# Attention scores and values of 16 groups: the next group's load cut into 14 issues spread over the step

## What is computed

```
scores = einsum('bqhd,bkhd->bhqk', Q, K) / sqrt(16)      # Q, K, V: (2, 2048, 16, 16)
scores = where(causal, scores, -inf)
attn   = softmax(scores, axis=-1)
out    = einsum('bhqk,bkhd->bqhd', attn, V)
x_out  = x + attention_1(norm(x)) + layer(norm(x))        # the layer holds attention_2 and the experts
```

## Time and profile before

| | us |
|---|---|
| median of 3 runs | 2648.76 (2633.55 to 2656.8) |
| profiled execution, its own time | 2634.57 |
| its span | 2632.8 |
| stage B, first to last score matmul | 273.2 to 1939.6 |
| engines busy over the span | PE 86%, DVE 71%, ACT 57%, POOL 22% |

### The profile page before, as it was taken

How to read it: one execution, slowest core, us unless ns; L and a number is a source line. 1 busy time by engine, 2 the same in 40 slices (tenths; PEclk the granted TensorE clock), 3 DMA queues, 4 the chain that set the end, 5 groups by cost and what they waited for, 6 DMA issues and landing times. The chain is left out here.

```text
span 2632.8 us, 45311 instructions
## 1 busy us (share of the span) xinstructions
PE 2277.3 (86%) x15785; PEld 1263.7 (48%) x15785; DVE 1866.1 (71%) x5760; ACT 1507.5 (57%) x3172; POOL 576.3 (22%) x490
## 2 busy tenths in 40 slices
PE   5986899999999999999999999999948512999994
PEld 3553344444444434444444444444426502899994
DVE  3536787978878889889888789797605642666662
ACT  2541576767767777777677677676840101445551
POOL 0001101010110110110100000100003265677775
PEclk9995798988989889989889899898978755999997
DMA  5994805415244154253252441541124403566663
GB/s 174 290 244 149 189 6 70 51 26 67 34 50 58 18 68 53 30 67 47 38 67 29 56 58 26 67 53 24 19 63 146 128 27 123 127 141 142 128 130 86
DMA packets 153968, 221.68 MB, mean 84 GB/s; under 512 B 57204, under 2 KB 116158, under 8 KB 145328
## 3 DMA queue, kind: packets, MB, share of 16 engines
q1 hardware_dynamic: 137136, 199.99, 38.3%
q0 software_dynamic: 16640, 19.25, 5.1%
HBM read 139.22 MB, written 89.39 MB: 87 GB/s over the span
## 5 line engine op out<-in xcount | busy, mean ns | idle before, releaser
L659 ACT ACTIVATE probs<-s_banks 128x512 f32<-128x512 f32 (+3 forms) x2560 | 1185.3, 538 | 442.8 <-PE s_banks L610 284.4
L696 DVE TENSOR_REDUCE rowmax<-m_banks 128x1 f32<-128x512 f32 x1536 | 967.0, 683 | 100.5 <-PE m_banks L621 93.4
L610 PE MATMUL s_banks<-qs,ks 50*128 50x512 f32 (+3 forms) x2560 | 872.5, 443 | 69.1 <-DMA qs<-mrows 53.3
L621 PE MATMUL m_banks<-ks,qs 48*128 48x512 f32 (+3 forms) x2560 | 839.6, 451 | 26.1 <-PEq L86 20.4
L639 PE MATMUL v_bank<-probs,vs 128*32 128x512 f32 (+3 forms) x5120 | 650.8, 583 | 1.1 <-ACT probs L659 0.4
L610 PEld LDWEIGHTS s_banks<-qs,ks 50*128 50x128 f32 x2560 | 422.7, 196 | 460.7 <-ACT probs L659 373.2
L693 DVE CUSTOM_DVE_ANT_0 unused<-m_banks,c_maskq 128x128 bf16<-128x128 f32 (+3 forms) x1024 | 465.9, 486 | 151.1 <-issue 147.8
L621 PEld LDWEIGHTS m_banks<-ks,qs 48*128 48x128 f32 x2560 | 417.8, 200 | 305.5 <-DVE rowmax L696 143.9
L552 POOL CAST nparts<-negmax 128x16 fp32r<-128x16 f32 x64 | 12.7, 198 | 1328.0 <-DVE negmax L702 1328.0
L1327 PE MATMUL e_banks<-w_parts,hid_parts 128*128 128x256 f32 x1536 | 188.8, 284 | 1.3 <-DVE hid_parts L1246 0.7
L1327 PEld LDWEIGHTS e_banks<-w_parts,hid_parts 128*128 128x128 f32 x1536 | 185.5, 192 | 2.0 <-DVE hid_parts L1246 1.1
(11 more groups left out here) (172 smaller groups left out, 1712.2 us busy)
## 6 DMA issues: line engine op xcount, KB each, us to landing
w<-in_L_ffn_fc_w SPq DMA_DIRECT2D x32, 1024.0 KB
qs<-q_scratch SPq DMA_DIRECT2D x96, 256.0 KB, 14.5
ks<-k_scratch SPq DMA_DIRECT2D x96, 256.0 KB, 16.2
q_scratch<-parts SPq DMA_DIRECT2D x64, 256.0 KB, 4.6
k_scratch<-parts SPq DMA_DIRECT2D x64, 256.0 KB, 4.5
xin_scratch<-rden POOLq DMA_DIRECT2D x16, 528.0 KB, 26.8
xin<-xin_scratch SPq DMA_DIRECT2D x16, 528.0 KB
v_scratch<-vt SPq DMA_DIRECT2D x16, 512.0 KB, 7.7
```

The lines of the kernel that those rows point to most:

```text
L610: ins = pe.matmul(bank, ks[rows, slot, h // 2, k * P:(k + 1) * P], qs[rows, slot, h // 2, q * CH + first:(q + 1) * CH], start=True, stop=n ...
L621: pe.matmul(room(("M", NM * group + n))[:, 0:width], qs[rows, slot, h // 2, t * P:(t + 1) * P], ks[rows, slot, h // 2, c * CH:c * CH + wid ...
L659: act.activation(probs[:, n % PR, 0:width], s_banks[:, (NS * group + n) % SRING, 0:width], ACT.Exp, scale=SCALE).then_inc(p_ready, 1)
L696: dve.tensor_reduce(out, scores, AX.X, ALU.max).then_inc(m_used, 1)
```

## The change

The load's one entry in the order becomes 14, at key tiles 1 to 14, each of which issues one of the same 14 DMAs, in the same order and through the same queue. The wait for `p_used` stays ahead of the first. Stage A's load of group 0 issues its 14 pieces in one go, as before.

```diff
+PIECES = 14
+
+def load_piece(queue, g, n, drams, keep):
     q_dram, k_dram, v_dram = drams
     qs, ks, v_in, loaded = keep
-    slot = g % SLOTS
-    for half in range(2):
-        for n in range(3):
-            at = slice(half * HALF + n * HD, half * HALF + (n + 1) * HD)
...
-            sp.dma_start(qs[at, slot].bitcast(F32), q_rows).then_inc(loaded[slot], 16)
-            sp.dma_start(ks[at, slot].bitcast(F32), k_rows).then_inc(loaded[slot], 16)
...
+    slot, half, place = g % SLOTS, n // 6, n // 2 % 3
+    if n < 12:
+        dram, rows, part = ((q_dram, qs, (0, 0, 1)), (k_dram, ks, (0, 1, 0)))[n % 2]
+        at = half * HALF + place * HD
+        queue.dma_start(rows[at:at + HD, slot].bitcast(F32),
+                        dram[part[place], g].rearrange("(a b) r t -> b r a t", b=2)[half]).then_inc(loaded[slot], 16)
+    else:
+        values = v_dram[g // (B * HG), g // HG % B, :, :, g % HG * (GH * HD):(g % HG + 1) * (GH * HD)]
+        tiles = slice((n - 12) * (S // P // 2), (n - 11) * (S // P // 2))
+        queue.dma_start(v_in[:, slot, tiles], values[:, tiles]).then_inc(loaded[slot], 16)
...
-                    load_group(sp, 0, (q_dram, k_dram, v_dram), keep)
+                    for n in range(PIECES):
+                        load_piece(sp, 0, n, (q_dram, k_dram, v_dram), keep)
...
-        if n == LOAD_AT and g + 1 < G:
-            order.append(("L", g + 1, 0))
+        if LOAD_AT <= n < LOAD_AT + PIECES and g + 1 < G:
+            order.append(("L", g + 1, n - LOAD_AT))
...
-            def load(g):
-                if g >= SLOTS:
+            def load(g, n):
+                if n == 0 and g >= SLOTS:
                     sp.wait_ge(p_used, AHEAD + NT * (g - SLOTS + 1))
-                load_group(sp, g, (q_dram, k_dram, v_dram), keep)
+                load_piece(sp, g, n, (q_dram, k_dram, v_dram), keep)
...
-                        load(group)
+                        load(group, n)
```

More of the change, by code:

```diff
@@ L55 @@
 SLOTS = 2
-def load_group(sp, g, drams, keep):
+PIECES = 14
+def load_piece(queue, g, n, drams, keep):
     q_dram, k_dram, v_dram = drams
     qs, ks, v_in, loaded = keep
-    slot = g % SLOTS
-    for half in range(2):
-        for n in range(3):
-            at = slice(half * HALF + n * HD, half * HALF + (n + 1) * HD)
-            q_rows = q_dram[(0, 0, 1)[n], g].rearrange("(a b) r t -> b r a t", b=2)[half]
-            k_rows = k_dram[(0, 1, 0)[n], g].rearrange("(a b) r t -> b r a t", b=2)[half]
-            sp.dma_start(qs[at, slot].bitcast(F32), q_rows).then_inc(loaded[slot], 16)
-            sp.dma_start(ks[at, slot].bitcast(F32), k_rows).then_inc(loaded[slot], 16)
-    tiles = v_dram[g // (B * HG), g // HG % B, :, :, g % HG * (GH * HD):(g % HG + 1) * (GH * HD)]
-    for n in range(0, S // P, S // P // 2):
-        sp.dma_start(v_in[:, slot, n:n + S // P // 2], tiles[:, n:n + S // P // 2]).then_inc(loaded[slot], 16)
+    slot, half, place = g % SLOTS, n // 6, n // 2 % 3
[8 more added lines that the diff above has]
+        queue.dma_start(v_in[:, slot, tiles], values[:, tiles]).then_inc(loaded[slot], 16)
 def stage_a(nc, x, scratch, const, keep):
```

## The result

The changed kernel takes 2554.3 us (median of 4, 2536.9 to 2557.5) against 2641.2 us (2629.7 to 2656.8): a ratio of 0.9672, interval 0.9628 to 0.9716, or 87 us less. The forecast was 2530, the range 2490 to 2605.

A forecast was written before the change was run, and what follows sets the result against it. Bound: late rows of maxima, held behind the load in SP's queue, making PE wait at tile 16 and costing clock. Steps 1 to 14 save 106.7 us, step 0 saves 2: 2634.6 - 108.7 = 2525.9, stated as 2530, range 2490 to 2605.

The forecast's parts named there:

- Rows of tile 16: Steps 1 to 14: rows of maxima issued at +20.8 in 4.90 us, so the 42 us of waits at tile 16 go.
- The load's landing: Next group's load complete at +39, ahead of its first M matmul at +41.7 in tile 17; slack 2.7 us.
- A step at full clock: Steps 1 to 14 without the wait: 37.9 + 56.4 = 94.3 us, taken as 94.5.
- The clock in steps 1 to 14: Clock falls in half of the steps, some 11 us low, 0.4 us lost per us: 2.2 us a step.
- Step 0: Beside POOL's fill, 11.3 us of waiting become 9 at the next group's first M: a gain of 2 us.
- Step 15, the term put at nothing: Last step, which loads nothing: its time was to stay as profiled, adding no gain or loss.
- Rival N: Steps 1 to 14: the gap alone caused the clock's fall, so none remains; 94.5 us a step, 2495 us; chance 0.17.
- The row of step 8: Evidence cited for Rival N: in step 8 the first low-clock window lies inside the wait at tile 16.
- B: Narrow tiles 13 to 15 bring the clock down every step, some 15 us: 100.5 us a step, about 2580; chance 0.20.
- C: Load lands some us late, so the wait moves to the next group's first M: about 2635 or 2594 us; chance 0.07.
- D: Values' pieces still need 25 us to land, first M waits 12 us each step: slower, 2788 us; chance 0.04.

The follow-up runs named there:

- second experiment: Changed kernel with all 12 pieces of queries and keys at tile 1 and only the two values' pieces behind the rows, at tile 9: 2559.3 us, ratio 0.9723.
- first experiment: Changed kernel with eight pieces issued together at key tile 1 and six at tile 9, nothing spread: 2543.5 us, ratio 0.9666.
- third experiment: Changed kernel with all 14 pieces of the load issued behind the rows, at tile 9: 2814.6 us (one run).
- fourth experiment: The changed kernel unaltered, run again for another profile: 2543.8 us, ratio 0.9633.

## Why the prediction was right, and where it was off

*Rows of tile 16, right, by a row misread in part.* Issued at +20.8 in 5.0 us, 42 us of waits gone. The prediction compared the row of 16 issues in the earlier trace rows (21.86 us) with 8 in 4.90. But the 16 are the rows of two chunks, the second eight wait until +37 for their own copy, and in step 15, where nothing holds them, they take 21.34 us as well. What shows that SP was held is the first issue alone, in the kernel before (step 2, then step 3):

```profile
515.04 12.58 SPq L480 DMA_DIRECT2D qs<-mrows  x1
...
609.67 1.05 SPq L72 DMA_DIRECT2D v_in<-v_scratch  x2
618.60 14.59 SPq L480 DMA_DIRECT2D qs<-mrows  x1
```

Both issues end at +35.4, just behind the landing of the eleventh piece (+34.8 in step 2), and the other seven follow, so that the last row goes out at +39.8. In step 3 the values' pieces go out in 1 us and the rows bear all of the hold. That it takes the values' pieces was inferred; the second experiment shows it, and the first that no spreading is needed.

*The load's landing, right.* +39.5 for my +39, the first M at +41.5 for my +41.7. The load was in time in every step, but not always with 2 us to spare: in step 3 it landed at +41.6 (issue at 610.2 and 12.9 us, start 581.5), too late by 0.1 us for a first M at +41.5; no wait came of it because the low clock had put that M off to +43.1. In the first experiment's step 3 it was +41.3 against a first M at +41.5. The third experiment shows the price beyond.

*A step at full clock, right.* 94.2 us; the sum gave 94.3 and I took 94.5.

*The clock in steps 1 to 14, too small.* In the first profile the low time is 99 us, 7.1 a step, for my 5.5 (half of the steps by 11 us). At 41 us lost over 14 x 94.2, 0.42 for each us, the rate was right. Ten of 14 steps had a fall, not seven, since there is a second place, behind tile 19 at +49, that no step of the kernel before had shown. So 97.1 us a step for my 96.7: 6 us. In the second profile (the fourth experiment) 12 of 14 steps had a fall, with 143 us of low time, 10.2 a step: 98.3 us a step, 22 us over the sum. The term was mis-sized, by little in one execution and by a factor of nearly two in the other.

*Step 0.* The wait became 8.1 us for my 9; the gain was 0.5 us for my 2, and 5 in the second profile.

*Step 15, the term put at nothing.* "Step 15 and the other stages stay" took one profiled execution for the rule. I had read its 3.4 us fall and used it for the others, but did not ask what a longer one would cost there. In four of the twelve profiles of kernels other than the one of before, its clock was low for 50 us or more (one of them had step 15 itself altered), in two of the kernel before for 3.4 us each; what decides this stays open. In the first profile this made 23.2 of the 31.7 us by which the execution fell short of my sum (108.7 against 77.0); 6 came from the clock, 1.5 from step 0 and 1.0 from the other stages. In the second, 20 us above my sum, step 15 had no part: the clock of steps 1 to 14 made 22, the other stages 1, and step 0 gave back 3. Both executions lost to the clock most of what the sum lacked, the first in step 15, the second in steps 1 to 14.

*The rivals.* Rival N (no falls once the gap is gone: 2495) is what the advice of the Trainium skill ("TensorE: Matmul & The Clock Gate", section "Why this matters for your kernels") gave. The measurements differ: in the fourth experiment every step from 3 to 15 fell with no gap ahead of it. The kernel before had shown it too. In step 1 the wait is from 424.9 to 427.5, and all of it is at the low clock, behind a window at 1.00 and with PE busy throughout:

```profile
421.40:424.80 3.40, 3.40 (x40) 2.71 (x40) 3.10 (x30) 2.63 (x11) 0.42 (x2) 1.00 0.99 140
424.90:427.50 2.60, 0.00 (x0) 0.00 (x0) 1.22 (x8) 0.13 (x1) 0.00 (x0) 0.50 0.01 3
```

So the wait cannot have brought the clock down there. In nine of the 14 steps it fell at +38.1 to +38.6, within 0.4 us of the wait's beginning at +38.2. The row of step 8 that the prediction held for N is one of them. With tiles 14, 15 and 19 filled, the time is 2493.6; that this is N's figure is chance, as it holds 10 us or more from POOL's fill and 12 matmuls a step that N did not have. B had the right place, the tiles ahead of tile 16; it said every step, some 15 us and 100.5 us a step, and the second profile came near it with 12 steps of 14, 12 us each and 98.3. C and D did not come.

## What to carry to other kernels

Look in the timeline of the issuing engine for issues that take 10 us where others take half a us: the queue is closed, and small urgent transfers should be issued ahead of the piece that closes it. A merged row of many issues does not show this; narrow the window to the first of them. When a short PE wait goes, count the low-clock time behind it too, and then look at what stands just ahead of each fall: here 12 superfluous matmuls a step, at under 0.1 us each, removed them. Where runs of one kernel spread by 20 us, a term "stays as it is" from a single profile is not safe.

## What was not expected of the hardware

The clock fell in stretches where the PE row shows no idle time over 0.3 us, at two fixed places: behind tiles 14 and 15, and behind tile 19. (That row counts a matmul as busy from start to modelled end; how full the array is does not show in it.) Putting 8 matmuls of 512 columns at the first place lengthened a step by 0.6 us and saved about 30 us in all; 4 more at the second, with POOL's fill moved, left steps 1 to 14 without a fall. Once low, the clock came back after 3.4 to 27 us in most steps, but in step 15 it stayed down for 54.6 us, and in the run with added matmuls through all of the 91.3 us that were left of the step, with the PE row busy throughout. A load of 12 pieces of 32 rows of 8 KB did not hold up SP for long (0.42 us an issue at the median, 1.5 at most in the second experiment); with two pieces of 256 KB in rows of 256 bytes behind them an issue took 10 to 15 us. That it is the many short rows that fill the queue is the likely reading, not a tested one: no run varied the length of the rows alone.
